# Expert index read during the up-projection, three expert loads on ScalarE's queue, class-row gates moved by one place

## The chip, the cores and the metric

The kernel runs on one core of one Trainium2 chip. The metric is device time in microseconds, taken as the median of the runs. The core's engines are TensorE (PE in the profile, with PEld for its weight loads), VectorE (DVE), ScalarE (ACT), GpSimd (POOL) and SyncE (SP). Each follows its own queue and waits on semaphores for the others.

## What is computed

Eight images of 256 by 256 give, after a wavelet stage, 8 x 257 tokens of width 256 (256 image rows and one class token an image). They pass one attention layer with a dense MLP, and then a routed layer. Of the last one this much matters here:

```python
logits = silu(x @ rw1 + rb1) @ rw2 + rb2          # 8 experts
k_logits, k_index = top_k(logits, 2)
k_prob = softmax(k_logits)
for e in range(8):                                 # w1[e]: 256x1024, w2[e]: 1024x256, float32
    we = sum(where(k_index == e, k_prob, 0))
    out += we[:, None] * (silu(x @ w1[e] + b1[e]) @ w2[e] + b2[e])
```

## The kernel before

**The routing steps.** A hand-written program for each engine handles the tokens in eight groups of 256 rows (g = 0 to 7), with step g of `routing_step` running the dense MLP of group g, the router of group g-1 and the gates of group g-2. Within step g TensorE transposes finished rows (`xm_T`), multiplies the MLP's second matrix (`mlp_out`, two tiles of 128 rows, each of 8 matrix products that the profile counts as 16 MATMULs), transposes the next rows (`x1_T`), and puts small matrix products in between: `ranks(g-2)` counts how many earlier rows chose each expert. `ranks` waits for a mask that VectorE makes in `choose`. VectorE then runs `settle`, which reads the ranks and, in `gates`, waits for the half-tangents that ScalarE makes in `gate_halves`. The eight class rows are a ninth, small group with the index B = 8. They are handled in step g = 3: `ranks(B)` on TensorE, `gate_halves(B)` on ScalarE, `choose(B)` and `settle(B)` on VectorE, and after these on VectorE `choose(1)` and `settle(1)`.

**The routed tiles.** GpSimd scatters every row with its gate to a region of its expert in memory (`scatter`, L778). VectorE then works out tables: for each of 40 tiles of 128 rows the owner (its expert, `owner_i`), the place of its rows (`row_i`), and how many expert loads must have landed (`need_i`). SP loads the rows of tile i into one of two buffers (`load_rows`, L645 and L646). TensorE turns them (`rows_T`, L2146), multiplies by w1 (`up`, 32 MATMULs of 128x128, in two halves c = 0 and c = 1), and, once ScalarE has applied the silu to both halves, by w2 (`down`, 16 MATMULs). VectorE scales the result (`tile_out`, L1354 and L1358), GpSimd adds it to the output in memory (`add_rows`, L820), and once an add has landed VectorE reads the slots and gates of a later tile (`rows_in`, L1347 and L1348), which raises `slot_ready`. SP waits for this before the next load of rows. TensorE's order in step i is `up(i+1)`, `rows_T(i+2)`, `down(i)`; the rows of tile j are loaded after `rows_in(j-2)`.

**Reading a table.** An engine that needs an entry of a table reads it into a register, in its own queue: TENSOR_LOAD, register operations and a check in the trace. TensorE does it twice ahead of `down` (the owner at L2163; the need at L550, for the wait of `wait_for_expert`), VectorE for the same tile in `weights_in`, and SP once ahead of each load of rows (L645).

**The expert weights.** Twelve loads of 1 MB (w1 and w2 of experts 0 to 5) are issued by SP in the routing steps, w1 of expert 6 after the last MLP product. The last three (w2 of expert 6, both of expert 7) are issued by SP just after the rows of tiles 0 and 1 (L606, L602, L606).

Of the kernel before, what the change touches and what calls it, by code (L numbers as in the profile page):

```python
# [25 lines left out]
P = 128  # L26
B, IMG = 8, 256
# [4 lines left out]
HID = 4 * D  # L32
E = 8
KD = D // P
KH = HID // P
T = 2
# [54 lines left out]
def build(nc, t):  # L91
# [3 lines left out]
    with ExitStack() as ctx:  # L95
# [451 lines left out]

        def wait_for_expert(eng, i):

            need = eng.value_load(need_i[0:1, bass.ds(i, 1)], min_val=LOW_LOADED, max_val=ALL_LOADED)  # L550
            eng.wait_ge(experts_loaded, need)
# [9 lines left out]
        def _(sp):  # L561
# [39 lines left out]
            def load_first(e):  # L601
                sp.dma_start(experts[:, e, 0:KD * HID].rearrange("p (k n) -> p k n", k=KD),  # L602
                             t["L0_ffn_w1"][e].rearrange("(k p) n -> p k n", p=P)).then_inc(experts_loaded, 16)

            def load_second(e):
                sp.dma_start(experts[:, e, KD * HID:EXPERT].rearrange("p (k n) -> p k n", k=KH),  # L606
                             t["L0_ffn_w2"][e].rearrange("(k p) n -> p k n", p=P)).then_inc(experts_loaded, 16)

            for e in range(E - 2):
                load_first(e)  # L610
                load_second(e)
# [20 lines left out]
            load_first(E - 2)  # L632
            sp.wait_ge(scat1, 16 * 2 * (T * B // 2))
            sp.wait_ge(scat0, 16 * 2 * (T * B // 2))
            sp.wait_ge(c_scat, 16 * 2)
            sp.wait_ge(idle_stored, 16)
            sp.wait_ge(tables_ready, 1)
            loaded = [xs_loaded0, xs_loaded1]

            def load_rows(i, par, ahead):  # L640

                if ahead:
                    sp.wait_ge(xsT_ps, i - 1)
                    sp.wait_ge(slot_ready, i - 1)
                row = sp.value_load(row_i[0:1, bass.ds(i, 1)], min_val=0, max_val=E * REGION)  # L645
                sp.dma_start(xs[par], xs_d[bass.ds(row, P), :]).then_inc(loaded[par], 16)  # L646
            load_rows(0, 0, False)
            load_rows(1, 1, False)

            sp.wait_ge(lg_ps, B)  # L650
            load_second(E - 2)
            load_first(E - 1)
            load_second(E - 1)
            with sp.Fori(0, MOE_TILES // 2 - 1) as it:
                load_rows(2 * it + 2, 0, True)
                load_rows(2 * it + 3, 1, True)
# [726 lines left out]
        def _(act):  # L1383
# [173 lines left out]
            def routing_step(g, par):  # L1557
# [11 lines left out]
                xm_T(g - 1, 1 - par)  # L1569
                if g + 1 < B:  # L1570
                    x1_T(g + 1, 1 - par)
                if g == 3:
                    gate_halves(B)
# [42 lines left out]
            rows_T(1, 1)  # L1616
            hidden_rows(0, 0)
# [16 lines left out]
        def _(pe):  # L1634
# [429 lines left out]
            def routing_step(g, par):  # L2064
# [26 lines left out]
                if g == 3:  # L2091
                    ranks(B)
                mlp_out(g, par, 0, mlp_use, range(0, 4))
                if g == 2:
                    class_sum()
                mlp_out(g, par, 0, mlp_use, range(4, KH))
# [52 lines left out]
            def up(i, par):  # L2149

                pe.wait_ge(w1_ready, i + 1)
                pe.wait_ge(xsT_sb, i + 1)
                after(pe, hT_sb, KH * (i - 1))
                for c in range(2):
# [7 lines left out]
            def down(i, par):  # L2162
                e = pe.value_load(owner_i[0:1, bass.ds(i, 1)], min_val=0, max_val=E - 1)  # L2163
                wait_for_expert(pe, i)
# [10 lines left out]
            def expert_step(i, par, turns):  # L2175

                if not isinstance(i, int) or i + 1 < MOE_TILES:
                    up(i + 1, 1 - par)
                if not isinstance(i, int) or i + 2 < MOE_TILES:
                    rows_T(i + 2, par, turns + 1)  # L2180
                down(i, par)
# [32 lines left out]
```

## Time and profile before

| what | value |
|---|---|
| median of 3 runs | 775.46 us (774.49 to 777.62) |
| profiled execution, its own time | 775.04 us |
| its span in the trace | 773.3 us |
| PE busy | 698.7 us, 90% of the span |
| DVE, ACT, POOL busy | 338.9, 294.4, 289.1 us |
| PE's share of the chain that ended last | 74% |
| granted TensorE clock, mean | 0.948 |

A busy share is an average over stages: TensorE is the busiest engine, and what the others do matters only where it waits for them. Durations in the text are of the profiled execution. Times of the trace count from the start of the span.

### The profile page before, as it was taken

What the parts mean: (1) busy time and instruction counts of PE and PEld (TensorE: products, weight loads), DVE (VectorE), ACT (ScalarE), POOL (GpSimd) and SP (SyncE); (2) the same over time, 40 slices, a digit from 0 to 9 for tenths busy, and PEclk for the clock granted to TensorE, in tenths of its full rate; (3) what the DMA queues carried; (4) which work ended last, traced back from release to release, by engine and by line L of the source; (5) the groups of instructions that cost most, each with busy time, mean ns of one, the idle gap of its engine ahead of it and who ended that gap; (6) DMA issues with size and microseconds to landing.
All of it is one profiled execution on the core that took longest, in us unless ns stands there. A gap on an engine that the chain in (4) does not pass through costs nothing.

```text
span 773.3 us, 14754 instructions
## 1 busy us (share of the span) xinstructions
PE 698.7 (90%) x4607; PEld 614.0 (79%) x4608; DVE 338.9 (44%) x1006; ACT 294.4 (38%) x762; POOL 289.1 (37%) x324
## 2 busy tenths in 40 slices
PE   0887999999999999899999648999999999999994
PEld 0756888899887786788888547989998999999893
DVE  6576667664524544455554442232333233232320
ACT  0433655556432544345443213332323333332320
POOL 7022866666751534344440421222322222232222
PEclk9978999999679999899999859999999999999998
DMA  9515999600000891001110451221222122122210
GB/s 224 186 23 111 288 275 279 151 0 1 1 1 0 311 372 41 29 22 35 43 43 15 166 194 41 34 40 27 31 38 34 31 34 35 23 35 40 35 21 0
DMA packets 53221, 63.96 MB, mean 83 GB/s; under 512 B 6348, under 2 KB 48768, under 8 KB 53008
## 3 DMA queue, kind: packets, MB, share of 16 engines
q1 hardware_dynamic: 43616, 53.76, 24.3%
q0 software_dynamic: 8112, 9.04, 7.1%
q10 hardware_dynamic: 1456, 0.68, 0.4%
q8 instruction: 21, 0.34, 0.2%
q14 instruction: 16, 0.13, 0.0%
HBM read 31.01 MB, written 31.38 MB: 81 GB/s over the span
## 4 chain that ended last, share of the span: by engine, by line
PE 74%; DVE 9%; DMA 5%; issue 4%; ACT 3%; POOL 3%; SPq 1%; POOLq 0%; DVEq 0%; ACTq 0%
PE bank L1636 71%; DMA arena<-in_L_tok_Wa 2%; DMA dense<-routed_rows 1%; DMA h<-arena 1%; DVE arena L995 1%; POOL routed_rows L778 1%; ACT dense L1612 1%; POOL small L545 1%; PE bank L1814 1%; DVE small L524 1%; POOL arena L727 1%; PE bank L2146 1%; PE bank L1668 1%; DVE dense L537 1%; ACT arena L1531 1%
## 5 line engine op out<-in xcount | busy, mean ns | idle before, releaser
L1636 PE MATMUL bank<-arena,dense 128*128 (+2 forms) x1408 | 308.3, 391 | 9.0 <-ACT dense L1612 6.6
L1636 PEld LDWEIGHTS bank<-arena,dense 128*128 128x128 f32 (+1 forms) x1408 | 247.0, 193 | 49.0 <-issue 13.8
L820 POOL DMA_INDIRECT out_tokens<-dense,slot_ids x40 | 77.6, 1940 | 238.5 <-DVE dense L1358 230.7
L1612 ACT ACTIVATE dense<-bank,small 128x128 f32<-128x128 f32 x320 | 91.3, 369 | 197.6 <-PE bank L1636 197.6
L1636 PEld LDWEIGHTS bank<-dense 128*128 128x128 f32 x1280 | 150.9, 194 | 1.9
L1636 PE MATMUL bank<-dense 128*128 128x128 f32 x1280 | 151.0, 277 | 0.0
L1636 PE MATMUL bank<-dense,arena 128*128 128x256 f32 (+2 forms) x688 | 110.9, 363 | 1.0 <-ACT arena L1445 0.7
L1636 PEld LDWEIGHTS bank<-dense,arena 128*128 128x128 f32 (+2 forms) x688 | 86.3, 194 | 17.9 <-issue 4.5
L727 POOL TENSOR_TENSOR arena<-arena 128x512 f32<-128x512 f32 x64 | 80.3, 1279 | 42.0 <-ACT arena L1465 42.0
L1531 ACT ACTIVATE arena<-bank,small 128x256 f32<-128x256 f32 x128 | 53.7, 471 | 84.3 <-PE bank L1636 84.2
L1636 PE MATMUL bank<-arena 128*128 128x34 f32 (+7 forms) x756 | 81.9, 302 | 3.5 <-ACT arena L1531 1.9
L1636 PEld LDWEIGHTS bank<-arena 128*128 128x128 f32 (+4 forms) x756 | 74.5, 177 | 12.3 <-ACT arena L1531 4.0
L1336 DVE COPY dense<-arena 128x2048 f32 x40 | 51.6, 1290 | 62.4 <-PE bank L1636 53.2
L1464 ACT ACTIVATE arena<-bank 128x512 f32<-128x512 f32 x64 | 38.6, 603 | 56.8 <-DVE arena L1069 56.8
L1347 DVE COPY small<-dense 128x1 f32 x40 | 6.2, 154 | 89.7 <-DMA out_tokens<-dense,slot_ids 88.5
L1354 DVE TENSOR_TENSOR dense<-bank,x 128x256 f32<-128x256 f32 x40 | 17.0, 425 | 64.6 <-PE bank L1636 64.6
L1069 DVE TENSOR_SCALAR arena<-bank 128x512 f32<-128x512 f32 x64 | 39.7, 682 | 2.7 <-PE bank L1636 2.1
L1465 ACT ACTIVATE arena<-arena 128x512 f32<-128x512 f32 x64 | 40.8, 637 | 0.0
L778 POOL DMA_INDIRECT routed_rows<-arena,place x28 | 27.6, 987 | 34.3 <-DVE place L1222 27.7
L544 POOL TENSOR_SCALAR small<-small 128x2 f32<-128x2 f32 (+1 forms) x28 | 6.3, 224 | 86.8 <-DVE small L528 86.7
L2146 PE MATMUL bank<-small,dense 128*128 128x128 f32 x80 | 15.9, 282 | 14.2 <-DMA dense<-routed_rows 14.2
L1604 ACT COPY dense<-bank 128x256 f32<-128x256 f32 x40 | 15.5, 389 | 17.1 <-PE bank L2146 17.1
(235 smaller groups left out, 549.5 us busy)
## 6 DMA issues: line engine op xcount, KB each, us to landing
routed_rows<-x SPq DMA_DIRECT2D x8, 2385.0 KB, 26.4
arena<-in_L_ffn_w SPq DMA_DIRECT2D x16, 1024.0 KB, 12.0
dense<-routed_rows SPq DMA_DIRECT2D x40, 132.5 KB, 2.1
arena<-in_x SPq DMA_DIRECT2D x4, 512.0 KB, 6.9
arena<-in_L_attn_w SPq DMA_DIRECT2D x2, 1024.0 KB
out_tokens<-h SPq DMA_DIRECT2D x8, 256.0 KB, 3.2
h<-arena SPq DMA_DIRECT2D x13, 128.0 KB
dense<-in_L_ffn_rw SPq DMA_DIRECT2D x1, 1024.0 KB, 9.2
```

The source lines that it names most:

```text
L727: pool.tensor_tensor(dst, dst, lin[i % 4], ALU.add).then_inc(f_sum, 1)
L778: pool.indirect_dma_start(out=xs_d[:, :], out_offset=bass.IndirectOffsetOnAxis(ap=idx, axis=0), in_=(c_pay if tail else rows_of(g, par))[0 ...
L820: pool.indirect_dma_start(out=sums[:, :], out_offset=bass.IndirectOffsetOnAxis(ap=slot_ids[par][:, 0:1], axis=0), in_=y[par], in_offset=No ...
L1069: dve.tensor_scalar(feature_rows(par, i), psF[i % 4][:, :], 0.0, None, ALU.min).then_inc(f_neg, 1)
L1336: dve.tensor_copy(w1now[par].rearrange("p k n -> p (k n)").rearrange("p (o n) -> p o n", o=1), experts[:, bass.ds(e, 1), 0:KD * HID]).then ...
L1354: link(dve.tensor_tensor(ybias[par].rearrange("p (o n) -> p o n", o=1), psAT[par][:, 0:D].rearrange("p (o n) -> p o n", o=1), b2bc[:, bass ...
L1464: act.activation(lin[i % 4], psF[i % 4][:, :], ACT.Relu).then_inc(f_read, 1)
L1465: act.activation(feature_rows(par, i), feature_rows(par, i), ACT.Exp).then_inc(f_exp, 1)
L1531: ins = act.activation(dst[:, 2 * i + m, 0:n], psF[i % 2][:, m * IMG:m * IMG + n], func, bias=bias[:, 2 * i + m:2 * i + m + 1])
L1612: act.activation(hT[par][:, k, :], psUP[par][c][:, P * m:P * m + P], ACT.Silu, bias=b1now[par][:, k:k + 1]).then_inc(hT_sb, 1)
L1636: return pe.matmul(out, lhsT, rhs, start=start, stop=stop, **kw)
L2146: ins = pe.transpose(psT[:, k * P:(k + 1) * P], xs[par][:, k * P:k * P + P], ident)
```

## The change

There are three edits.

TensorE reads only the owner of a tile, and does it between the two halves of the up-projection of the next tile. It no longer reads the need of the tile, nor waits for it. VectorE still does both, before it copies the tile's w1.

On SP the row indices are read ahead of the waits and not behind them. The loads of w2 of expert 6 and of both matrices of expert 7 leave SP and are issued from ScalarE's queue, after `rows_T(1, 1)`.

In routing step 3 ScalarE's `gate_halves(B)` goes ahead of `x1_T(4)`, and TensorE's `ranks(B)` moves from the front of `mlp_out` to the middle of its first tile.

```diff
@@ SP
             sp.wait_ge(experts_loaded, LOW_LOADED)
-            load_first(E - 2)
+            load_first(sp, E - 2)
+            loaded = [xs_loaded0, xs_loaded1]
+
+            def row_of(i):
+
+                return sp.value_load(row_i[0:1, bass.ds(i, 1)], min_val=0, max_val=E * REGION)
+
+            def load_rows(par, row):
+                sp.dma_start(xs[par], xs_d[bass.ds(row, P), :]).then_inc(loaded[par], 16)
+
+            def load_ahead(i, par):
+
+                row = row_of(i)
+                sp.wait_ge(xsT_ps, i - 1)
+                sp.wait_ge(slot_ready, i - 1)
+                load_rows(par, row)
+            sp.wait_ge(tables_ready, 1)
+            first_rows = [row_of(i) for i in range(2)]
+            sp.wait_ge(idle_stored, 16)
+            sp.wait_ge(c_scat, 16 * 2)
+            sp.wait_ge(scat0, 16 * 2 * (T * B // 2))
             sp.wait_ge(scat1, 16 * 2 * (T * B // 2))
-            sp.wait_ge(scat0, 16 * 2 * (T * B // 2))
-            sp.wait_ge(c_scat, 16 * 2)
-            sp.wait_ge(idle_stored, 16)
-            sp.wait_ge(tables_ready, 1)
-            loaded = [xs_loaded0, xs_loaded1]
-
-            def load_rows(i, par, ahead):
-
-                if ahead:
-                    sp.wait_ge(xsT_ps, i - 1)
-                    sp.wait_ge(slot_ready, i - 1)
-                row = sp.value_load(row_i[0:1, bass.ds(i, 1)], min_val=0, max_val=E * REGION)
-                sp.dma_start(xs[par], xs_d[bass.ds(row, P), :]).then_inc(loaded[par], 16)
-            load_rows(0, 0, False)
-            load_rows(1, 1, False)
-
-            sp.wait_ge(lg_ps, B)
-            load_second(E - 2)
-            load_first(E - 1)
-            load_second(E - 1)
+            for i in range(2):
+                load_rows(i, first_rows[i])
             with sp.Fori(0, MOE_TILES // 2 - 1) as it:
-                load_rows(2 * it + 2, 0, True)
-                load_rows(2 * it + 3, 1, True)
+                load_ahead(2 * it + 2, 0)
+                load_ahead(2 * it + 3, 1)
@@ ScalarE, routing step
                 xm_T(g - 1, 1 - par)
+                if g == 3:
+                    gate_halves(B)
                 if g + 1 < B:
                     x1_T(g + 1, 1 - par)
-                if g == 3:
-                    gate_halves(B)
@@ ScalarE, routed tiles
             rows_T(0, 0)
             rows_T(1, 1)
+            act.wait_ge(scat0, 16 * 2 * (T * B // 2))
+            act.wait_ge(scat1, 16 * 2 * (T * B // 2))
+            act.wait_ge(lg_ps, B)
+            load_second(act, E - 2)
+            load_first(act, E - 1)
+            load_second(act, E - 1)
             hidden_rows(0, 0)
@@ TensorE, routing step
-                if g == 3:
-                    ranks(B)
                 mlp_out(g, par, 0, mlp_use, range(0, 4))
                 if g == 2:
                     class_sum()
+                if g == 3:
+                    ranks(B)
                 mlp_out(g, par, 0, mlp_use, range(4, KH))
@@ TensorE, routed tiles
-            def down(i, par):
-                e = pe.value_load(owner_i[0:1, bass.ds(i, 1)], min_val=0, max_val=E - 1)
-                wait_for_expert(pe, i)
+            def owner_of(i):
+
+                return pe.value_load(owner_i[0:1, bass.ds(i, 1)], min_val=0, max_val=E - 1)
+
+            def down(i, par, e):
+
                 pe.wait_ge(hT_sb, KH * (i + 1))
@@ TensorE, expert_step
                 if not isinstance(i, int) or i + 1 < MOE_TILES:
-                    up(i + 1, 1 - par)
+                    up(i + 1, 1 - par, range(0, 1))
+                e = owner_of(i)
+                if not isinstance(i, int) or i + 1 < MOE_TILES:
+                    up(i + 1, 1 - par, range(1, 2))
                 if not isinstance(i, int) or i + 2 < MOE_TILES:
                     rows_T(i + 2, par, turns + 1)
-                down(i, par)
+                down(i, par, e)
```

How TensorE's queue stands in the routed tiles, from `up(1)` to the first product of `down(0)`, before (L2146 is `rows_T`, the loads at L2163 and L550 are the two table reads, `dense` holds rows and tables, `arena` the experts):

```order
L1636 MATMUL bank<-dense 128x128 [waits xsT_sb,w1_ready]
L1636 MATMUL bank<-dense 128x128 x15
L2146 MATMUL bank<-small,dense 128x128 [waits xsT_sb,xs_loaded0]
L2146 MATMUL bank<-small,dense 128x128
L2163 TENSOR_LOAD dense
L2163 ISA x2
L550 TENSOR_LOAD dense
L550 ISA x2
L1636 ISA [waits hT_sb,experts_loaded]
L1636 MATMUL bank<-arena,dense 128x256
```

The same place in the changed kernel (L1644 is the matrix product, L2154 `rows_T`, L2173 the read of the owner):

```order
L1644 MATMUL bank<-dense 128x128 [waits xsT_sb,w1_ready]
L1644 MATMUL bank<-dense 128x128 x7
L2173 TENSOR_LOAD dense
L2173 ISA x2
L1644 MATMUL bank<-dense 128x128 x8
L2154 MATMUL bank<-small,dense 128x128 [waits xsT_sb,xs_loaded0]
L2154 MATMUL bank<-small,dense 128x128
L1644 ISA [waits hT_sb]
L1644 MATMUL bank<-arena,dense 128x256
```

One read stood behind the turn of the rows and stands now in the middle of the up-projection, the other is gone with its wait, and nothing is left between the turn and `down` but the wait for `hT_sb`.

How SP's queue stands from the read of the first row index to the last expert load, before:

```order
L645 TENSOR_LOAD dense [waits idle_stored,c_scat,tables_ready,scat0,scat1]
L645 ISA x2
L646 ISA
L646 DMA dense<-routed_rows 128x265
L645 TENSOR_LOAD dense
L645 ISA x2
L646 ISA
L646 DMA dense<-routed_rows 128x265
L606 DMA arena<-in_L_ffn_w 128x8x256 [waits lg_ps]
L602 DMA arena<-in_L_ffn_w 128x2x1024
L606 DMA arena<-in_L_ffn_w 128x8x256
```

The same place in the changed kernel, up to the first read in the loop over tiles:

```order
L637 TENSOR_LOAD dense [waits tables_ready]
L637 ISA x2
L637 TENSOR_LOAD dense
L637 ISA x2
L640 ISA [waits scat0,scat1,c_scat,idle_stored]
L640 DMA dense<-routed_rows 128x265
L640 ISA
L640 DMA dense<-routed_rows 128x265
L656 UNCONDITIONAL_BRANCH
L656 ISA
L637 TENSOR_LOAD dense
L637 ISA x2
```

The reads wait for the tables alone, the row loads for the scatters, and no expert load stands ahead of the rows of tile 2.

TensorE's queue in routing step 3 before, from the turn of finished rows to `x1_T` (L1949 and L1940 are the two turns):

```order
L1949 MATMUL bank<-small,arena 128x128 x3
L1636 MATMUL bank<-small 128x24 [waits c_mask]
L1636 MATMUL bank<-small 128x16
L1636 MATMUL bank<-small 128x8
L1636 MATMUL bank<-dense,arena 128x256 [waits h1_ready,m_sb]
L1636 MATMUL bank<-dense,arena 128x256 x7
L1940 MATMUL bank<-small,dense 128x128 [waits x1T_sb,xmT_sb,xh_ready]
```

And in the changed kernel:

```order
L1957 MATMUL bank<-small,arena 128x128 x3
L1644 MATMUL bank<-dense,arena 128x256 [waits h1_ready,m_sb]
L1644 MATMUL bank<-dense,arena 128x256 x3
L1644 MATMUL bank<-small 128x24 [waits c_mask]
L1644 MATMUL bank<-small 128x16
L1644 MATMUL bank<-small 128x8
L1644 MATMUL bank<-dense,arena 128x256 x4
```

The three products of `ranks(B)` with their wait for `c_mask` stand four products of the MLP later.

## Rows read from the trace of the kernel before

**Rows 1.** Chain that ended last, routed tiles: start us, us, what.

```profile
475.94 7.04 PE bank L1636 x48
...
747.97 10.76 PE bank L1636 x64
```

**Rows 2.** Timeline, TensorE alone, routed tiles: start us, us, instructions, [idle before <-releaser].

```profile
604.30 3.62 PE L1636 MATMUL bank<-arena,dense 128*128 x16
...
611.33 0.38 PE L2146 MATMUL bank<-small,dense 128*128 128x128 f32 x2
612.16 3.72 PE L1636 MATMUL bank<-arena,dense 128*128 x16 [0.45 <-ACT dense L1612]
```

**Rows 3.** TensorE's table reads by line, two tiles: ns min/median/max, first to last start us.

```profile
L2163 PEldq TENSOR_LOAD <-dense x1: 301/301/301, 602.4 to 602.4; - x1
...
L2163 PEldq TENSOR_LOAD <-dense x1: 303/303/303, 610.4 to 610.4; - x1
...
L550 PEldq SEQ_ASSERT  x1: 18/18/18, 611.8 to 611.8; - x1
```

**Rows 4.** Timeline (first row) and SP's row loads by line, same tile.

```profile
607.14 0.14 DVE L1348 CAST slot_ids<-dense 128x1 uint32<-128x1 f32 x1
...
L646 SPq DMA_DIRECT2D dense<-routed_rows x1: 338/338/338, 608.2 to 608.2; - x1
...
DMA to landing us min/median/max: 2.1/2.1/2.1
```

**Rows 5.** Timeline, TensorE alone, two tiles further on.

```profile
665.17 3.62 PE L1636 MATMUL bank<-arena,dense 128*128 x16
...
672.42 3.62 PE L1636 MATMUL bank<-arena,dense 128*128 x16
```

**Rows 6.** Timeline, all engines, start of the routed tiles.

```profile
452.68 1.49 SPq L646 DMA_DIRECT2D dense<-routed_rows  x2
...
455.59 0.37 ACT L1604 COPY dense<-bank 128x256 f32<-128x256 f32 x1 [15.91 <-PE bank L2146]
...
456.10 0.66 PE L2146 MATMUL bank<-small,dense 128*128 128x128 f32 x2 [0.55 <-DMA dense<-routed_rows]
...
456.55 9.08 PE L1636 MATMUL bank<-dense 128*128 128x128 f32 x64
```

**Rows 7.** Chain that ended last, start of the routed tiles.

```profile
451.69 0.49 SPq L645
...
456.86 9.77 DMA dense<-routed_rows
467.12 1.31 issue
```

**Rows 8.** Expert loads on SP: by line, and from the timeline of SP's queue.

```profile
L606 SPq DMA_DIRECT2D arena<-in_L_ffn_w x2: 433/451/469, 454.2 to 455.3; - x2
...
255.46 6.17 SPq L602 DMA_DIRECT2D arena<-in_L_ffn_w  x1
```

**Rows 9.** Timeline, all engines, routing step 3.

```profile
305.63 0.83 PE L1636 MATMUL bank<-small 128*128 128x24 f32 x6 [1.15 <-DVE small L1174]
...
313.40 0.14 DVE L1184 TENSOR_SCALAR small<-small 8x1 f32<-8x1 f32 x1 [6.15 <-ACT small L1554]
...
316.36 0.99 PE L1636 MATMUL bank<-small 128*128 128x24 f32 x6 [2.48 <-DVE small L1174]
...
320.54 1.68 PE L1636 MATMUL bank<-arena,dense 128*128 128x256 f32 x7
```

**Rows 10.** Timeline, TensorE alone, the same place in routing step 4.

```profile
336.66 3.72 PE L1636 MATMUL bank<-dense,arena 128*128 128x256 f32 x16
...
342.38 0.73 PE L1636 MATMUL bank<-small 128*128 128x24 f32 x6
...
344.78 1.46 PE L1636 MATMUL bank<-arena,dense 128*128 128x256 f32 x6
```

**Rows 11.** Windows: us, busy of PE, PEld, DVE, ACT, POOL, PEclk, DMA share, GB/s.

```profile
307.00:308.00 1.00, 1.00 (x4) 0.81 (x3) 0.22 (x2) 0.00 (x0) 0.00 (x0) 0.50 0.00 0
```

More of the change, by code:

```diff
@@ L546, in root, with load_first, load_second @@
                                ).then_inc(answered, 1)
+        def load_first(eng, e):
+            eng.dma_start(experts[:, e, 0:KD * HID].rearrange("p (k n) -> p k n", k=KD),
+                          t["L0_ffn_w1"][e].rearrange("(k p) n -> p k n", p=P)).then_inc(experts_loaded, 16)
+        def load_second(eng, e):
+            eng.dma_start(experts[:, e, KD * HID:EXPERT].rearrange("p (k n) -> p k n", k=KH),
+                          t["L0_ffn_w2"][e].rearrange("(k p) n -> p k n", p=P)).then_inc(experts_loaded, 16)
         def wait_for_expert(eng, i):
@@ L599, in _ @@
             sp.wait_ge(catt_moved, 16 * 4)
[L601 to L607, printed above, removed]
             for e in range(E - 2):
-                load_first(e)
-                load_second(e)
+                load_first(sp, e)
+                load_second(sp, e)
             stored = [h1_stored0, h1_stored1]
@@ L2147, in rows_T, with up @@
                 ins.then_inc(xsT_ps, 1)
[L2149 to L2154, printed above, removed]
+            def up(i, par, cs=range(2)):
+                if 0 in cs:
+                    pe.wait_ge(w1_ready, i + 1)
+                    pe.wait_ge(xsT_sb, i + 1)
+                    after(pe, hT_sb, KH * (i - 1))
+                for c in cs:
                     for m in range(4):
```

## The prediction

> **What bounds the kernel now.** The profiled execution took 775.04 us; its span is 773.30 and 1.74 lies around it. The median is 775.46, so 0.42 above. I read the chain of waits first. Over the routed tiles it is TensorE's matrix products and almost nothing else: the piece that begins with `down(1)` starts at 475.94 and the one with `down(37)` at 747.97 [rows 1]. The first starts 0.17 late, since its first matmuls are put to the turn of rows, so 36 tiles take 272.2 us, 7.56 each. Then I took TensorE's own timeline, to see whether it is full. It is not: from one `down` to the next there are 7.86 us in one case (604.30 to 612.16), with TensorE idle for 0.45 just before the second [rows 2]; and two tiles further on there is a pair that needs only 7.25 [rows 5]. So 0.31 us a tile is no work. The profile puts that idle time to a ScalarE activation, but the activation that `down` needs belongs to a tile whose silu was finished long before; the names there are inferred. What is the wait? The reads of the tables show it. In the tile with the hole, TensorE's queue begins the first read at 610.4, and the check behind the second ends at 611.8 [rows 3], 0.3 before `down`, although the array had reached the turn of the rows at 611.33 [rows 2]. In the tile without one, the first read begins at 602.4 [rows 3], 1.7 before the turn (604.30 less 0.22). So the queue runs ahead of the array by about 1.7 us, and the two reads take 1.3 to 1.4 of it: just enough. In the tile with the hole it was held at the wait for the rows: VectorE frees the slot at 607.14+0.14, SP issues the load at 608.2, and it lands 2.1 later, at 610.3 [rows 4], where the read begins. Two things together make the hole: rows that land 1.0 before their turn, and 1.4 us of reads behind them.
>
> Two more places stand out in the chain: the start of the routed tiles, where TensorE waits for one load of 9.77 us and then 1.31 us for "issue" [rows 7], and routing step 3, where it waits 1.15 and 2.48 us for VectorE's masks [rows 9].
>
> **The change, part by part.**
>
> *Routed tiles.* Behind the turn nothing is read any more, so `down` can follow at once if the rows have landed. SP's read is ahead of its wait: of the 0.9 us between 607.28 and 608.2 [rows 4] about 0.75 goes (the same read took from 451.69 to about 452.5 at the start, rows 7 give 0.49 for its load alone), the rows land near 609.5, and the array turns them at 611.2. The one read that stays is put in the middle of the up-projection. Its cost from below is 0, hidden by the 1.7 us that the queue is ahead. From above it is half of the 1.31 us that two reads cost where nothing hid them [rows 7], 0.66 a tile. I take 0: the nearest row is the one at 602.4, where the queue was ahead by 1.7 while the array was busy with the same up-projection. After the read it is still ahead by about 1.0, and it has the second half of the up-projection in which to get its lead back. What comes next as a bound is the loop over VectorE, GpSimd and the add in memory: slot freed to slot freed must stay below 7.25, and the tiles that already run at 7.25 [rows 5] show that it can. The gain is 272.2 - 36 x 7.25 = 11.2 us. If that cover were gone, it would be lost and more; that is the first rival below.
>
> *Start of the routed tiles.* SP's read leaves the path: the first load of rows goes out at about 451.9 instead of 452.68 [rows 6, 7], 0.8 earlier. The second turn then waits for ScalarE's copy of the first, which ended at 455.96 [rows 6] and will end near 455.2, so it starts at 455.2 instead of 456.10, and `up(0)` at 455.65 instead of 456.55: 0.9 gained. From there to `down(0)` it was 467.12 + 1.31 - 456.55 = 11.88 us. It now needs the two up-projections, 9.08 [rows 6], and 0.2 for the turn, if the rows of tile 2 are there. Their load was issued at 456.86, behind three expert loads, and took 9.77 [rows 7]. Now nothing stands ahead of it on SP, and it can go once the first turn is done and slot 0 is free, near 455.0; ScalarE issues its loads only after its second copy, near 456.2. 2.1 us later, at 457, the rows are there, and they are needed at 464.7. So 2.6 us gained, 3.5 with the 0.9. The three issues cost ScalarE between 0.43 and 0.47 for those of w2 [rows 8]; with 1.5 in all it is free at 457.7, and its first silu waits for half of `up(0)`, a fourth of the 9.08, so not before 455.65 + 2.27 = 457.9. The bound from above is 6.17 for an issue when the queue is full [rows 8], the fifth of twelve loads issued one behind the other. I take 0, as the three that are moved took 0.5 each on SP. Rows of tile 3 are issued near 463.5 among the expert loads, and are needed at 472. The last expert loads are wanted only by the tiles of experts 6 and 7, the last of the 40.
>
> The Trainium skill speaks against this part (DMA: Bandwidth & Descriptors, "Issuing engines are not separate DMA queues"): loads from different engines run on the same 16 DMA engines and interleave, and a second issuing engine saves only issue time. By that, the rows would still come late if they met the expert loads. The trace has no case of both queues at once. I hold that here the order in time decides, not the queue, and give the case a chance below.
>
> *Class-row gates.* In step 3 TensorE is done with the turn at 305.63 - 1.15 = 304.48 and reaches the router's products at 320.54 [rows 9]: 16.1 us. In step 4 the same work from the MLP's first product takes 344.78 - 336.66 = 8.12 [rows 10]. Step 3 has one `ranks` more, 0.7. The rest, 7.2, is the two waits (3.6) and a slow clock: after the first wait the granted clock goes from full to half (0.50 between 307 and 308) [rows 11]. In the changed order the first four MLP products fill the time until VectorE's class mask is there (it came at 305.6): they end at 306.3, and `ranks(B)` follows with no wait. VectorE then waited 6.15 us for the half-tangent until 313.40 [rows 9], because ScalarE had `x1_T(4)` in front of it. Now it comes ahead of it, well before VectorE asks. So VectorE, which was at that wait 1.6 after `ranks(B)` began, is there at 307.9 and goes on at once; the next mask was ready 316.36 - 313.40 = 2.96 after that point, so 310.8 now. `ranks(1)` falls due in TensorE's order at 304.48 + 5.72 (its place in step 4, 342.38 - 336.66) + 0.7 = 310.9. No wait, or 0.1. Without holes I expect the clock to stay full. From 304.48 it is then 8.8 us instead of 16.1: 7.2 gained. The lower bound is the waits alone, 3.6, if the clock falls all the same. I take 7.2, since TensorE had no hole of 1 us left that would precede a fall. The later steps follow TensorE, so the gain is kept to the end.
>
> **Sum.** 11.2 + 3.5 + 7.2 = 21.9. From 775.04 that is 753.1, and against the median 753.5.
>
> **The rivals.**
>
> *The read in the middle stalls the array (slower).* If the queue is not ahead at that point, each of 39 tiles pays 0.66, and 0.1 for the overlap of two groups of matmuls that a hole costs (3.72 against 3.62 [rows 2]): 29.6 us. With the other gains, 775.46 - 21.9 + 29.6 = 783.2. It decides from a lead of under 0.6 us. The row at 602.4 speaks against it. Chance 0.03.
>
> *The hole stays in part.* The loop over the add in memory, not SP, sets when rows land, and half of the 11.2 stays lost: 759.1. Against it stands that rows would have to come 1.7 us later than I expect. Chance 0.09.
>
> *The clock falls in step 3 anyway, or VectorE is late with the mask:* 3.6 less, 757.1. Chance 0.10.
>
> *Expert loads and rows meet at the start.* Rows of tile 2 land as late as before less 0.9, 465.7, and `down(0)` begins at 466: 1.1 less, 754.6. Chance 0.06. The rest of the start (the two reads) is won either way. This is what the sentence of the Trainium skill would make of it.
>
> *ScalarE's queue fills up.* Three issues at 6.17 hold ScalarE to 474.7, and its first silus come 15 us late: 13 to 15 less, 767. Chance 0.03.
>
> *The change does nothing measurable:* the holes come from something I don't see in the trace and step 3 is repaid later. 775. Chance 0.02.
>
> The forecast as summed has 0.67.
>
> **How the numbers follow.** The likeliest case gives 753.5, its own range 751 to 756. For the whole I take 750.5, one more hole or wait gone that I did not see, to 761.5, which holds the partly kept holes together with a lost clock gain in part. What lies above, 767 and more, has 0.08. A measurement of this kernel tells about 0.5% (3.9 us) from no change. All cases but the last and the stall are faster by more: 0.95 faster; 0.02 within 0.5%; 0.03 slower.
>
> **What would show it.** Right: `down` to `down` 7.25 us in nearly all tiles, and no idle before `down`; the read of the owner takes its 0.3 us while the array goes on; row loads issued within 0.3 us of the freed slot; `down(0)` at about 9.3 us behind `up(0)`; in step 3 no wait of VectorE for a half-tangent, no PEclk of 0.50, and the router's products 8.8 us behind the turn. Wrong: a hole between the halves of the up-projection, rows of tile 2 that land after 464, expert loads that hold ScalarE for several us, or in step 3 a wait of TensorE for `mask_ready` of over 0.5 us, with the clock down behind it.

## The result, and the profile after

| what | before | after |
|---|---|---|
| median | 776.19 us of 4 runs (774.49 to 777.62) | 752.05 us of 4 runs (751.83 to 753.68) |
| ratio, with its 95% interval | | 0.9694 (0.9669 to 0.972) |
| profiled execution, its span | 775.04, 773.3 us | 751.93, 750.2 us |
| PE busy | 698.7 us, 90% | 689.4 us, 92% |
| granted TensorE clock, mean | 0.948 | 0.953 |

The change makes the kernel 24.1 us faster, where 21.9 was predicted. The span can be cut at places that both traces have, and the stages add up to its 23.1:

| stage | before | after | difference | predicted |
|---|---|---|---|---|
| to the turn of finished rows in step 3 | 303.86 | 304.35 | +0.5 | 0 |
| from there to the router's products of step 3 | 16.68 | 9.21 | -7.47 | -7.2 |
| from there until the last scatter has landed | 131.13 | 130.88 | -0.25 | 0 |
| from there to `down(1)` | 24.10 | 19.69 | -4.41 | -3.5 |
| `down(1)` to `down(37)`, 36 tiles | 272.20 | 260.82 | -11.38 | -11.2 |
| from there to the end | 25.33 | 25.25 | -0.08 | 0 |

The places of the cuts that no other row shows, in the kernel before (TensorE's timeline, then the chain) and in the changed one (chain):

```profile
303.86 0.63 PE L1949 MATMUL bank<-small,arena 128*128 128x128 f32 x4
...
475.77 3.62 PE L1636 MATMUL bank<-arena,dense 128*128 x16
```

```profile
448.99 2.68 DMA routed_rows<-dense,place
```

```profile
442.00 2.44 DMA routed_rows<-dense,place
```

**Routed tiles.** The chain of the changed kernel (start us, us, what) answers to [rows 1]:

```profile
457.05 7.03 PE bank L1644 x48
464.29 7.03 PE bank L1644 x48
...
725.11 10.50 PE bank L1644 x64
```

From 464.29 to 725.11 there are 36 tiles in 260.82 us, 7.245 each. TensorE's timeline in one of them answers to [rows 2]:

```profile
580.05 3.62 PE L1644 MATMUL bank<-arena,dense 128*128 x16
583.51 3.73 PE L1644 MATMUL bank<-dense 128*128 128x128 f32 x32
587.08 0.38 PE L2154 MATMUL bank<-small,dense 128*128 128x128 f32 x2
587.29 3.62 PE L1644 MATMUL bank<-arena,dense 128*128 x16
```

From `down` to `down` it is 7.24 us, and none of the four rows shows an idle time before it. The owner's read in the same tile, by line, answers to [rows 3]:

```profile
L2173 PEldq TENSOR_LOAD <-dense x1: 301/301/301, 583.2 to 583.2; - x1
...
L2173 PEldq SEQ_ASSERT  x1: 18/18/18, 583.8 to 583.8; - x1
```

The read stands between the two halves of the up-projection. The array reaches the second half half-way from 583.51 to the turn at 587.08, at about 585.3, and the queue has begun the read at 583.2: it is 2.1 us ahead, and the read is over 1.5 us before it could hold anything up. What SP does with the rows, same tile (the last row holds for all 40 loads), answers to [rows 4]:

```profile
582.27 0.14 DVE L1350 CAST slot_ids<-dense 128x1 uint32<-128x1 f32 x1
...
L640 SPq DMA_DIRECT2D dense<-routed_rows x1: 333/333/333, 582.6 to 582.6; - x1
...
DMA to landing us min/median/max: 2.0/2.1/5.0
```

The load goes out 0.2 us after the slot is free (582.27 + 0.14), where it was 0.9 before. At the median of 2.1 it lands near 584.7, and the array turns the rows at 587.08: 2.4 us of cover instead of 1.0.

**Start of the routed tiles.** Timeline of the changed kernel, all engines, to be held against [rows 6, 7, 8]:

```profile
446.89 0.66 PE L2154 MATMUL bank<-small,dense 128*128 128x128 f32 x2 [11.57 <-DMA dense<-routed_rows]
...
448.55 8.28 PE L1644 MATMUL bank<-dense 128*128 128x128 f32 x64
...
448.88 0.40 ACTq L553 DMA_DIRECT2D arena<-in_L_ffn_w  x1
...
449.31 1.66 ACTq L549 DMA_DIRECT2D arena<-in_L_ffn_w  x1
...
451.00 0.49 ACTq L553 DMA_DIRECT2D arena<-in_L_ffn_w  x1
...
451.59 1.14 ACT L1614 ACTIVATE dense<-bank,small 128x128 f32<-128x128 f32 x4 [2.42 <-PE bank L1644]
...
456.67 0.38 PE L2154 MATMUL bank<-small,dense 128*128 128x128 f32 x2
...
456.88 3.62 PE L1644 MATMUL bank<-arena,dense 128*128 x16
```

The first turn of routed rows is at 446.89; the row of 448.55 is the pair of first up-projections, `up(0)` and `up(1)`. The third turn (456.67) and `down(0)` (456.88) follow them with no wait; the load of 9.77 us and the 1.31 us of issue are gone. From the first turn to `down(0)` it takes 9.99 us instead of 13.54. ScalarE's three issues take 2.6 us in all, and its first silu follows 0.1 behind the last of them; by the row it waited for TensorE's product, not for them. SP's loads of rows by line, for tiles 0 to 2 and for tile 3:

```profile
L640 SPq DMA_DIRECT2D dense<-routed_rows x3: 333/344/362, 444.7 to 447.7; - x3
...
DMA to landing us min/median/max: 2.1/2.1/2.2
```

```profile
L640 SPq DMA_DIRECT2D dense<-routed_rows x1: 333/333/333, 455.8 to 455.8; - x1
...
DMA to landing us min/median/max: 5.0/5.0/5.0
```

The rows of tile 2 are issued at 447.7, 1.2 ahead of the first expert load, and land in 2.2 or less. Those of tile 3, issued with the expert loads under way, take 5.0, which is the maximum of all 40.

**Step 3.** Timeline of the changed kernel, all engines, and a window over the place at which the clock had fallen, to be held against [rows 9, 11]:

```profile
306.54 0.73 PE L1644 MATMUL bank<-small 128*128 128x24 f32 x6
...
308.09 0.14 DVE L1186 TENSOR_SCALAR small<-small 8x1 f32<-8x1 f32 x1
...
311.11 0.79 PE L1644 MATMUL bank<-small 128*128 128x24 f32 x6
...
313.56 6.66 PE L1644 MATMUL bank<-arena,dense 128*128 128x256 f32 x30
```

```profile
306.00:308.00 2.00, 2.00 (x14) 1.85 (x13) 0.70 (x7) 0.00 (x0) 1.36 (x2) 1.00 0.00 0
```

Neither `ranks(B)` (306.54) nor VectorE at the half-tangent (308.09) nor `ranks(1)` (311.11) has an idle time of note in front of it, and the granted clock is 1.00 where it was 0.50.

### The profile page after: what moved, and what is told of

It reads as the page before. It is cut to its first block, busy times and chain, and to the rows that moved or that the text cites. A ratio compares the mean times of both kernels' runs of the same rounds, so it can differ in the third digit from the quotient of the medians.

```text
span 750.2 us, 14597 instructions
## 1 busy us (share of the span) xinstructions
PE 689.4 (92%) x4607; PEld 610.2 (81%) x4608; DVE 339.4 (45%) x1006; ACT 294.2 (39%) x762; POOL 289.0 (39%) x324
## 4 chain that ended last, share of the span: by engine, by line
PE 77%; DVE 8%; DMA 4%; issue 3%; POOL 3%; ACT 2%; SPq 0%; POOLq 0%; DVEq 0%; ACTq 0%
PE bank L1644 73%; DMA arena<-in_L_tok_Wa 2%; PE bank L2154 1%; DVE arena L997 1%; POOL routed_rows L780 1%; DMA h<-arena 1%; POOL small L545 1%; PE bank L1822 1%; DVE small L524 1%; POOL arena L729 1%; PE bank L1676 1%; DVE dense L537 1%; ACT arena L1533 1%; DVE arena L917 0%; DVE arena L920 0%
## 5 line engine op out<-in xcount | busy, mean ns | idle before, releaser
L1644 PE MATMUL bank<-arena,dense 128*128 (+2 forms) x1408 | 306.6, 389 | 1.1 <-ACT arena L1434 0.8
L1644 PEld LDWEIGHTS bank<-arena,dense 128*128 128x128 f32 (+1 forms) x1408 | 247.2, 193 | 36.7 <-ACT arena L1533 2.9
L1644 PEld LDWEIGHTS bank<-dense 128*128 128x128 f32 x1280 | 150.1, 193 | 1.9
L1644 PE MATMUL bank<-dense 128*128 128x128 f32 x1280 | 150.2, 276 | 0.0
L1644 PE MATMUL bank<-dense,arena 128*128 128x256 f32 (+2 forms) x688 | 108.0, 359 | 1.1 <-ACT arena L1447 0.7
L1644 PEld LDWEIGHTS bank<-dense,arena 128*128 128x128 f32 (+2 forms) x688 | 83.9, 192 | 17.1 <-issue 4.5
L1644 PE MATMUL bank<-arena 128*128 128x34 f32 (+7 forms) x756 | 81.7, 301 | 3.3 <-ACT arena L1533 1.9
L1644 PEld LDWEIGHTS bank<-arena 128*128 128x128 f32 (+4 forms) x756 | 74.4, 177 | 12.2 <-ACT arena L1533 4.0
L2154 PE MATMUL bank<-small,dense 128*128 128x128 f32 x80 | 15.8, 281 | 12.1 <-DMA dense<-routed_rows 11.6
L1663 PE MATMUL bank<-small,arena 48*128 48x48 f32 (+1 forms) x33 | 4.2, 309 | 19.4 <-DMA arena<-in_L_tok_Wa 18.3
```

The source lines that it names most:

```text
L1644: return pe.matmul(out, lhsT, rhs, start=start, stop=stop, **kw)
L2154: ins = pe.transpose(psT[:, k * P:(k + 1) * P], xs[par][:, k * P:k * P + P], ident)
```

## The experiments

Eleven kernels were run in three groups, each group beside the kernel before (medians 777.34 of 13 runs, 777.83 of 7, 775.10 of 7; 776.19 beside the changed kernel). "Loop" is `down(1)` to `down(37)`, 36 tiles, 272.20 in the kernel before and 260.82 in the changed one.

| kernel | median us | ratio to before | loop us |
|---|---|---|---|
| `gates_only` | 768.63 | 0.9891 (0.9843 to 0.994) | 271.56 |
| `pe_only` | 765.0 | 0.9834 (0.9786 to 0.9883) | 260.82 |
| `sp_reads_only` | 763.53 | 0.9819 (0.9772 to 0.9865) | 261.17 |
| `act_loads_only` | 774.21 | 0.9949 (0.9929 to 0.997) | 271.83 |
| `ranks_back` | 757.66 | 0.974 (0.9704 to 0.9775) | 260.82 |
| `halves_back` | 759.57 | 0.9762 (0.9717 to 0.9807) | 260.82 |
| `reads_3` | 753.59 | 0.9683 (0.9652 to 0.9714) | 260.82 |
| `reads_5` | 803.62 | 1.0332 (1.0291 to 1.0373) | 306.25 |
| `act_first` | 759.16 | 0.978 (0.9747 to 0.9813) | 260.82 |
| `sp_after_rows2` | 753.5 | 0.9707 (0.9675 to 0.974) | 260.82 |
| `need_behind` | 765.43 | 0.9842 (0.9792 to 0.9891) | 261.21 |

Over the stretch ahead of step 3, in which the kernels do not differ, the traces differ by up to 3.7 us (303.2 to 306.9), and the kernel before itself differs by 2.7 from group to group. So a comparison of two medians, above all of two groups, carries 1 to 3 us that are no edit's; lengths of stages inside a trace are sharper, and I go by them.

**1. Each part alone, on the kernel before.** The theory: three parts with prices of their own. The rival: the two parts at the routed tiles each cure the same hole.

`gates_only` is the kernel before with these two edits:

```diff
@@ ScalarE
+                if g == 3:
+                    gate_halves(B)
                 if g + 1 < B:
                     x1_T(g + 1, 1 - par)
-                if g == 3:
-                    gate_halves(B)
@@ TensorE
-                if g == 3:
-                    ranks(B)
                 mlp_out(g, par, 0, mlp_use, range(0, 4))
                 if g == 2:
                     class_sum()
+                if g == 3:
+                    ranks(B)
```

> The kernel before with the class-row gates moved and nothing else. Theory (two waits and a half clock go): step 3 shortens by 7.2 to 7.5 us, so about 769 against 776.2. Rival (only the waits go, the clock falls all the same): 3.6 us less, about 772.6.

768.63, 8.7 less than before. TensorE's timeline of `gates_only`, the turn and the router's products:

```profile
304.86 0.64 PE L1949 MATMUL bank<-small,arena 128*128 128x128 f32 x4
...
314.07 10.55 PE L1636 MATMUL bank<-arena,dense 128*128 128x256 f32 x48
```

Step 3 takes 9.21 us, as in the changed kernel. So the 7.5 us are this edit's and need none of the others.

`pe_only` is the kernel before with TensorE's edits at the routed tiles (the owner's read in the middle, the need's read and wait gone).

> The kernel before with TensorE's part alone (owner read in the middle of the up-projection, need neither read nor waited for on TensorE); SP reads behind its waits as before. Theory (a hole needs rows that land 1.0 us before their turn AND 1.4 us of reads behind them, either cure is enough): loop at 7.25 us a tile, 11.3 less, and 1.3 less at the start: about 763.5. Rival (late rows alone make the hole): the loop stays at 7.56, about 775.

765.0. The loop is at 260.82: all of its hole is gone, though SP still reads its index behind its wait. At the start the rows of tile 2 are still late. TensorE's timeline of `pe_only`:

```profile
469.31 0.44 PE L2146 MATMUL bank<-small,dense 128*128 128x128 f32 x2 [1.46 <-DMA dense<-routed_rows]
469.58 3.62 PE L1636 MATMUL bank<-arena,dense 128*128 x16
```

The turn waits for the load, but `down(0)` follows at once: the 1.31 us of the two reads are gone. From the first turn (457.31) to `down(0)` it is 12.27 instead of 13.54.

`sp_reads_only` is the kernel before with SP's reads ahead of its waits, the expert loads staying on SP:

```diff
-                if ahead:
-                    sp.wait_ge(xsT_ps, i - 1)
-                    sp.wait_ge(slot_ready, i - 1)
-                row = sp.value_load(row_i[0:1, bass.ds(i, 1)], min_val=0, max_val=E * REGION)
+                row = row_of(i)
+                sp.wait_ge(xsT_ps, i - 1)
+                sp.wait_ge(slot_ready, i - 1)
```

> The kernel before with SP's reads of the row index ahead of its waits; the three expert loads stay on SP in their place, TensorE reads as before. Theory (either cure is enough): rows land 0.75 earlier, the hole of 0.7 every second tile closes, 11 less, and 0.9 less at the start: about 764. Rival (TensorE's reads alone make the hole): only the 0.9, about 775.

763.53. The loop is at 261.17, although TensorE still has both reads behind the turn. The rows land some 0.7 us earlier, and the two reads fit into the queue's lead again. At the start they are still seen. The chain (first row) and TensorE's timeline of `sp_reads_only`:

```profile
452.62 2.13 DMA dense<-routed_rows
```

```profile
467.90 3.72 PE L1643 MATMUL bank<-arena,dense 128*128 x16 [1.32 <-ACT dense L1619]
```

The first load of rows is issued 0.23 after the last scatter (452.39); `down(0)` comes after 1.32 us of idle time. The profile names a ScalarE activation, but as in [rows 7] the two reads stand in this time, and nothing hid them.

`act_loads_only` is the kernel before with the three expert loads on ScalarE's queue (the helpers, moved and given the engine as an argument, are not shown):

```diff
@@ SP
-            sp.wait_ge(lg_ps, B)
-            load_second(E - 2)
-            load_first(E - 1)
-            load_second(E - 1)
@@ ScalarE
             rows_T(1, 1)
+            act.wait_ge(scat0, 16 * 2 * (T * B // 2))
+            act.wait_ge(scat1, 16 * 2 * (T * B // 2))
+            act.wait_ge(lg_ps, B)
+            load_second(act, E - 2)
+            load_first(act, E - 1)
+            load_second(act, E - 1)
```

> The kernel before with the last three expert loads issued from ScalarE after its second copy; all reads as before. Theory (the rows of tile 2 no longer stand behind the expert loads): they land about 2.1 us after issue in place of 9.8, and the first down comes 2.5 us sooner: about 773.7. Rival (loads of both queues share the engines, so the rows are as late as before): 776. The loop keeps its holes, 7.56 us a tile, in both.

774.21. The loop stays at 271.83. TensorE's timeline of `act_loads_only`, the first turn and `down(0)`:

```profile
458.41 0.66 PE L2148 MATMUL bank<-small,dense 128*128 128x128 f32 x2 [12.49 <-DMA dense<-routed_rows]
...
468.98 3.62 PE L1638 MATMUL bank<-arena,dense 128*128 x16
```

It takes 10.57 us instead of 13.54, 3.0 less. Both reads are still there, but `down(0)` has no wait: with the rows in time the reads are hidden here too.

The four gains are 8.7, 12.3, 13.8 and 3.1 us: 38.0, where the whole change gives 24.1. The loop shows most of the reason. TensorE's part takes 11.38 out of it and SP's part 11.03, and together they take 11.38. That is 11.0 of the 13.9 us too many. Another 1.3 is the start: from the last scatter to `down(1)` the three parts gain 1.41, 1.25 and 3.03 alone and 4.41 together. The rival holds: the hole had two causes, and either cure closes it.

**2. One part taken back, on the changed kernel.** The edits are the two halves of the diff of `gates_only`, reversed one at a time: `ranks_back` puts `ranks(B)` back to the front of `mlp_out`, `halves_back` puts `gate_halves(B)` back behind `x1_T(4)`.

> The changed kernel with ranks(B) on TensorE back ahead of the MLP's first product; ScalarE's move stays. Theory: TensorE waits some 1.2 us for the class mask; the next mask is not late. 753.2 if the clock stays full, up to 755.2 if it falls to half for some 4 us as it did before.

757.66, 5.6 more than the changed kernel (5.0 between the two traces), and above the 753.2 to 755.2 that I had expected. TensorE's timeline and a window of `ranks_back`:

```profile
305.98 0.83 PE L1644 MATMUL bank<-small 128*128 128x24 f32 x6 [1.15 <-DVE small L1176]
306.67 5.39 PE L1644 MATMUL bank<-dense,arena 128*128 128x256 f32 x16
```

```profile
307.00:308.00 1.00, 1.00 (x4) 0.82 (x3) 0.86 (x10) 0.00 (x0) 0.20 (x1) 0.50 0.00 0
```

The first wait of [rows 9] is back with its 1.15 us, and with it the half clock: the 16 MATMULs behind it take 5.39 us, where step 4 has 3.72 for as many [rows 10]. Step 3 takes 12.27, 3.06 more, within what I had put on it (1.2 to 3.2). Of the rest, 1.4 is a longer pair of first up-projections (9.69 instead of 8.28, see below).

> The changed kernel with gate_halves(B) on ScalarE back behind x1_T; TensorE's move stays. Theory: VectorE waits for the half-tangent until about 310.8, the next mask comes at 313.8 where 310.9 is wanted: 2.9 us of wait, and a fall of the clock on top: 755 to 757. Rival (TensorE's move alone does it): 752.

759.57, again above what I had expected (755 to 757). Of `halves_back`: VectorE's wait (us, number, longest), TensorE's timeline, and two windows.

```profile
DVE small L1186 <- ACT small L1556: 2.7, 1, 2.7
```

```profile
315.76 1.25 PE L1644 MATMUL bank<-small 128*128 128x24 f32 x6 [2.49 <-DVE small L1176]
316.86 3.76 PE L1644 MATMUL bank<-dense,arena 128*128 128x256 f32 x8
```

```profile
320.00:322.00 2.00, 2.00 (x6) 1.64 (x5) 1.18 (x3) 0.00 (x0) 1.69 (x2) 0.50 0.19 68
322.00:324.00 2.00, 2.00 (x9) 1.66 (x8) 0.25 (x2) 0.45 (x2) 1.39 (x3) 0.79 0.23 83
```

The second wait of [rows 9] is back: VectorE is late by 2.7 us, TensorE by 2.49, and eight MATMULs take 3.76 at half the clock. Step 3 takes 14.07, 4.86 more, and the half clock lasts beyond its end: the clock is back at 1.00 only by 324. At the first turn of routed rows the trace is 8.95 later, 2.0 of which were there ahead of step 3, so 2.1 came after the stage. Not all of it need be the hole's: from the router's products to the last scatter this trace takes 132.88 us, and the other twelve take 130.9 to 131.7. An estimate from the windows (half clock from 320.42 to about 322.8) gives the hole 1.2 of it. So the first hole, 1.15 us long, cost 3.06, and the second, 2.49 long, cost 4.86 and 1.2 to 2 behind it. In the kernel before, where both stand, they cost 7.47 together and 0.25 behind. The two edits of this part do not stand in for one another.

**3. How far the queue is ahead.** The first rival of the prediction would stall the array if the queue were under 0.6 us ahead. To find the edge, the read is repeated:

```diff
+                for _ in range(2):        # reads_3; range(4) in reads_5
+                    owner_of(i)
                 e = owner_of(i)
```

> The changed kernel with the owner read three times in the middle of the up-projection, so 2.0 us in place of 0.67. Theory (TensorE's queue is 2.2 us ahead of the array at that point: the read begins at 583.2, the second half of the up-projection at about 585.4): still hidden, 752. Rival (the read is only just hidden, lead of the 1.0 to 1.7 us that was seen at the turn of rows): 0.3 to 1.0 us a tile, 764 to 791.

753.59, and the loop at 260.82: there three reads are as free as one. By line, in one tile of `reads_3`:

```profile
L2173 PEldq TENSOR_LOAD <-dense x3: 302/302/303, 584.3 to 585.5; - x3
```

> The changed kernel with the owner read five times there, 3.35 us. Theory (lead of 2.2 us): a hole of about 1.1 us in each of 39 tiles: about 795. Rival (the queue can be further ahead if it has to): 752.

803.62, where I had expected about 795, and the loop at 306.25, 1.26 us more a tile (I had 1.1). The weight loads' timeline in `reads_5`:

```profile
610.51 1.86 PEld L1644 LDWEIGHTS bank<-dense 128*128 128x128 f32 x16 [1.18 <-issue]
```

The hole stands between the halves of the up-projection, as the rival had it. Five reads at 0.66 are 3.3 us, and 1.26 are seen, so about 2.0 are hidden, which is what three reads take. That agrees with the 2.1 us read from the trace above.

**4. Order in time or queue.** I had held that the rows of tile 2 come early because they are issued ahead of the expert loads, and not because these have another queue. `act_first` has both queues as in the changed kernel, but ScalarE issues ahead of its two copies, together with the first loads of rows:

```diff
-            rows_T(0, 0)
-            rows_T(1, 1)
+            act.wait_ge(experts_loaded, LOW_LOADED + 16)
             act.wait_ge(scat0, 16 * 2 * (T * B // 2))
             ...
             load_second(act, E - 1)
+            rows_T(0, 0)
+            rows_T(1, 1)
```

> The changed kernel with ScalarE's three expert loads moved ahead of its two copies, so that they are issued together with the rows of tiles 0 and 1 and some 2.6 us before those of tile 2: the order in time of the kernel before, on two queues. Theory A (what held the rows was their place behind 3 MB on one queue): rows of tile 2 land within 5 us of issue and the time is within 1 us of 752, but for ScalarE's issue time of about 2.5 us ahead of its first copy, which delays the up-projection by up to 2.4. Theory B (all queues share the same engines, so 3 MB ahead in time delay the rows wherever they are issued): rows of tile 2 land 8 to 10 us after issue, those of tiles 0 and 1 late as well, 754 to 758.

759.16, 7.1 more than the changed kernel by the medians of two groups. In the traces, from the last scatter to `down(1)`, it is 24.91 instead of 19.69, 5.2 more. Timeline and chain of `act_first`:

```profile
447.08 0.41 ACTq L553 DMA_DIRECT2D arena<-in_L_ffn_w  x1
...
447.53 0.62 ACTq L549 DMA_DIRECT2D arena<-in_L_ffn_w  x1
...
454.66 0.69 PE L2155 MATMUL bank<-small,dense 128*128 128x128 f32 x2 [2.68 <-DMA dense<-routed_rows]
```

```profile
447.72 6.90 DMA dense<-routed_rows
```

A load of rows that takes 2.1 us alone takes 6.90 when the expert loads of the other queue are under way, and `down(0)` begins at 464.59. ScalarE's issues end near 448.7, long before the rows, so they are not what is late. Loads of one queue delay those of another. The Trainium skill says that DMAs run on the same 16 DMA engines and interleave, whichever engine started them (DMA: Bandwidth & Descriptors, "Issuing engines are not separate DMA queues"), and the trace agrees.

The queue is not without effect, though. The rows of tile 2, issued at 452.1, took 5.1 us, where I had expected 8 to 10, and landed near 457.2, some 2 us ahead of the last expert load (issued at 448.17, 11.1 to landing). On one queue, in the kernel before, they took 9.77 and landed at 466.63, just behind the last expert load (issued at 455.31, 11.0 to landing).

`sp_after_rows2` is the other half: one queue, but the right order. The three loads are back on SP, behind the rows of tile 2 (their removal from ScalarE and the shorter loop that follows are not shown):

```diff
+            load_ahead(2, 0)
+            sp.wait_ge(lg_ps, B)
+            load_second(sp, E - 2)
+            load_first(sp, E - 1)
+            load_second(sp, E - 1)
+            load_ahead(3, 1)
```

> The changed kernel with the three expert loads back on SP, but issued behind the load of tile 2's rows. Theory (order in time decides, not the queue): rows of tile 2 land in 2 us, those of tile 3 stand behind the expert loads but are wanted only 15 us later: 752. Rival (the second queue is what helps): above 753.5.

753.5, and the loop at 260.82. The median lies just where theory (752) and rival (above 753.5) meet; the trace decides. TensorE's timeline of `sp_after_rows2`:

```profile
449.14 0.66 PE L2154 MATMUL bank<-small,dense 128*128 128x128 f32 x2 [11.76 <-DMA dense<-routed_rows]
...
460.61 3.62 PE L1644 MATMUL bank<-arena,dense 128*128 x16
```

`down(0)` again follows with no wait for rows. It is 11.47 behind the first turn, where the changed kernel has 9.99; 1.46 of that is a pair of first up-projections of 9.74 us. ScalarE's queue is not needed for the gain: that the rows of tile 2 go out first is enough.

**5. One read behind the turn.** On the kernel before, the owner's read goes to the middle (as in the change), and the need's read and wait stay behind the turn:

```diff
-            def down(i, par):
-                e = pe.value_load(owner_i[0:1, bass.ds(i, 1)], min_val=0, max_val=E - 1)
+            def down(i, par, e):
                 wait_for_expert(pe, i)
```

> The kernel before with TensorE's owner read moved to the middle of the up-projection, but the need still read and waited for behind the turn of rows. Theory (hole = what is read behind the turn, less what the rows are early): one read of 0.67 us in place of 1.4 leaves 0 to 0.1 of the hole of 0.7, and 0.65 less at the start: about 765. Rival (it is the wait on a register or its value that costs, not the time of the reads): the loop stays near 7.56, 775.

765.43, the loop at 261.21. TensorE's timeline of `need_behind` at the start:

```profile
470.61 3.71 PE L1636 MATMUL bank<-arena,dense 128*128 x16 [0.46 <-issue]
```

One read behind late rows is hidden in the loop (the rows land 1.0 before their turn, and a read takes 0.66), two are not; where the rows come last, as here, even one costs 0.46.

## Why the prediction was right

**Routed tiles** (11.2 predicted, 11.38 measured). Right in size and in cause. The hole needed both late rows and two reads: taking away either closed it (`pe_only`, and `sp_reads_only` but for 0.35 us). The read in the middle cost nothing; the lead that hides it is 2.0 to 2.1 us there, where I had 1.7 from the turn at the up-projection's end. The rival with a stall is real as a mechanism (`reads_5`), but it takes more than three reads. What the prediction did not say is that the two edits overlap: with SP's alone 11.03 us were there. The sum came out because it counted the hole once.

**Start of the routed tiles** (3.5 predicted, 4.41 measured). The first term holds: 0.77 between the last scatter and the first load of rows (0.24 instead of 1.01). From the first turn to `down(0)` 3.55 were gained. Of these, 0.80 is a shorter pair of up-projections (8.28 us instead of 9.08 with the same instructions), because the half clock ended sooner (near 450.6, 2.0 us into the pair, and near 460.3, 3.7 into it, in the kernel before); 2.75 is what I had put at 2.6. So one term was mis-sized, by 0.8, and it is one that the change does not set: the same pair took between 8.20 and 9.87 us in the kernels that were run. The cost of ScalarE's issues was taken as 1.5 us and was 2.6. That it stayed hidden, with 0.1 us to the first silu, is in part luck: the issues ended 2.9 us behind the start of `up(0)`, where the prediction had the first silu 2.27 behind it. The silu came 3.04 behind, since the first products ran at half clock, which the prediction had left out. The rows of tile 3 took 5.0 and were still there in time: issued at 455.8, turned at 463.91 (I had put their issue near 463.5).

**Class-row gates** (7.2 predicted, 7.47 measured). Right, and shown in its parts: 3.06 without TensorE's move, 4.86 without ScalarE's, each a wait and the half clock behind it. I had expected 8.8 from the end of the turn; 9.21 from its start is 8.6 on that scale (the turn takes about 0.6). After the stage, 0.25 more was gained, within what the traces differ by there. `halves_back` shows that a hole can also cost after its stage.

**The rivals.** That the clock falls anyway, that the hole stays in part and that nothing is gained are excluded by the traces. That rows and expert loads meet did not happen, because the rows of tile 2 went out 1.2 us ahead of ScalarE's first issue (447.7 against 448.88); `act_first` shows what it costs when they do, 5.2 us in its stage, and not the 1.1 that I had put on it, since it is then the rows of tiles 0 and 1 that are late. That ScalarE's queue fills up did not happen: the longest issue was 1.66 us. That a full queue was the reason for SP's 6.17 is not shown by any run; the trace shows only that the first four issues took 0.39 to 0.78, the fifth 6.17, and the later ones 0.65 to 4.46.

**Open.** Why the first up-projections of the routed tiles leave the half clock sooner in some traces than in others. In the changed kernel (windows, columns as in [rows 11]) it does so within 2.5 us of the first one's start:

```profile
450.00:451.00 1.00, 1.00 (x9) 1.00 (x8) 0.00 (x0) 0.00 (x0) 0.00 (x0) 0.71 0.67 136
451.00:452.00 1.00, 1.00 (x12) 1.00 (x11) 0.00 (x0) 0.41 (x2) 0.00 (x0) 1.00 1.02 353
```

`reads_3` and `sp_after_rows2`, with a like wait ahead of it (11.56 and 11.76 us against 11.57), took 1.6 and 1.5 us longer over the pair. The 1.5 us by which the medians of these two lie above the changed kernel is of this size, and is not put down to their edits, but for a small part in `reads_3`: between the halves of `up(1)` its weight loads are idle for 0.20 us behind the three reads. `ranks_back`, which changes nothing here, took 1.4 longer.

## What to carry to other kernels

A table read that stands behind a wait costs its time only if the wait ends late; find how far the engine's queue is ahead of its array (here 2 us), and put the read where the queue is ahead, not where it waits. Before a gain is added up from parts, ask whether two of them cure one hole: here 38.0 us of single gains made 24.1. For loads that compete, change the order in which they are issued; another queue alone did not keep them apart here.

## What the runs showed of the hardware

Two holes of TensorE in step 3 weighed more than their length: 1.15 us cost 3.06 (`ranks_back`), and 2.49 us cost 4.86 in the stage and 1.2 to 2 behind it (`halves_back`). After each the granted clock went to half (1.2 GHz).

The middle one of three expert loads took ScalarE 1.66 us to issue (1.31 in `act_loads_only`, 0.62 in `act_first`), where the outer ones took 0.40 and 0.49. I had expected 0.5 from SP's issues. It is neither always the middle one nor ScalarE alone: in `halves_back` the last took 1.06 and the middle one 0.61, and on SP, in `sp_after_rows2`, the last took 1.95.

Three 1 MB loads under way delayed a load of 128 rows from 2.1 us to 9.77 when it stood behind them on their queue, and to between 4.0 and 6.9 when it came from another queue (`act_first`).
